# Attention and feed-forward block: values in runs of three units, other work paced by TensorE's columns and VectorE's reads

## The reference, cut to what matters

```python
xn = layernorm(x)
q, k, v = heads(xn @ Wq.T + bq), heads(xn @ Wk.T + bk), heads(xn @ Wv.T + bv)   # 16 heads of 16
q, k = rope(q), rope(k)
att = softmax(where(tril, q @ k.T / 4, -inf))
attn = merge(att @ v) @ Wo.T + bo
prob = softmax(xn @ router_w.T + router_b)        # 16 blocks of 64 hidden units
mask = the 4 best blocks of each token
h = relu(where(mask, xn @ w1.T + b1, 0))          # 1024 hidden units
out = x + attn + (h @ w2.T + b2)
```

## Time and profile before

| what | value |
|---|---|
| median of 3 runs | 927.0 us (926.43 to 928.52) |
| profiled execution | 931.0 us |
| its span, first to last instruction | 929.2 us |
| mean granted TensorE clock | 0.984 |
| TensorE, matmuls | 881.8 us busy |
| VectorE | 547.9 us busy |
| ScalarE | 458.3 us busy |
| GpSimd | 281.6 us busy |

### The profile page before, as it was taken

The page is one execution under the profiler, slowest core; times in us unless marked ns, Lnnn a source line. Parts: engine busy times, 40 slices in busy tenths (PEclk is TensorE's granted clock), DMA queues, the critical chain, the costliest instruction groups (busy, mean ns, idle before and its releaser), DMA issues.

```text
span 929.2 us, 15131 instructions
## 1 busy us (share of the span) xinstructions
PE 881.8 (95%) x5440; PEld 498.9 (54%) x5440; DVE 547.9 (59%) x1728; ACT 458.3 (49%) x1065; POOL 281.6 (30%) x298
## 2 busy tenths in 40 slices
PE   4879999999999999999999999999999999999996
PEld 2546544543555645555555655555555555565554
DVE  5936755667777565565666656555555765655301
ACT  2511355556555554445563554545454654645562
POOL 4356042916540029265041007627200002000000
PEclk9979999999999999999999999999999999999999
DMA  8570401423331144230230224122240205000001
GB/s 296 190 203 20 118 3 47 137 71 69 95 114 43 28 138 137 70 71 4 91 113 2 70 71 113 50 75 63 70 132 8 70 24 138 2 3 1 3 1 46
DMA packets 45626, 69.65 MB, mean 75 GB/s; under 512 B 5104, under 2 KB 20336, under 8 KB 45552
## 3 DMA queue, kind: packets, MB, share of 16 engines
q1 hardware_dynamic: 45552, 68.69, 25.4%
HBM read 38.93 MB, written 29.75 MB: 74 GB/s over the span
## 4 chain that ended last, share of the span: by engine, by line
PE 82%; DVE 7%; issue 5%; DMA 2%; ACT 2%; POOL 1%; SPq 1%; ACTq 0%; DVEq 0%; POOLq 0%
PE o_bank L887 14%; PE s_bank L871 14%; PE m_bank L821 13%; PE m_bank L810 12%; PE s_bank L797 11%; PE s_bank L771 5%; PE m_bank L858 3%; PE s_bank L874 3%; PE s_bank L780 2%; PE m_bank L836 1%; DVE m_bank L1101 1%; PE s_bank L801 1%; POOL x_sb L525 1%; DMA k_st<-term_scratch 1%; DMA term_scratch<-pieces 1%
## 5 line engine op out<-in xcount | busy, mean ns | idle before, releaser
L678 ACT ACTIVATE probs<-s_bank 128x512 f32<-128x512 f32 (+3 forms) x768 | 342.6, 492 | 250.1 <-PE s_bank L874 184.3
L821 PE MATMUL m_bank<-k_st,q_st 96*128 96x512 bf16 (+3 forms) x768 | 249.8, 330 | 13.9 <-DVE row_max L1101 5.7
L871 PE MATMUL s_bank<-q_st,k_st 99*128 99x512 bf16 (+3 forms) x768 | 250.0, 331 | 3.8 <-ACT rope_sb L640 2.2
L1098 DVE TENSOR_REDUCE part_max<-m_bank 128x1 f32<-128x512 f32 x256 | 167.5, 687 | 88.8 <-PE m_bank L821 87.6
L1101 DVE CUSTOM_DVE_ANT_0 m_bank<-m_bank,tri,part_max 128x512 f32<-128x512 f32 (+3 forms) x256 | 131.8, 556 | 68.9 <-PE m_bank L821 67.2
L887 PE MATMUL o_bank<-probs,v_sb 128*17 128x512 f32 (+3 forms) x1536 | 161.6, 494 | 0.0
L1101 DVE CUSTOM_DVE_ANT_0 m_bank<-m_bank,tri 128x512 f32<-128x512 f32 (+3 forms) x256 | 121.6, 512 | 54.3 <-PE m_bank L821 52.9
L871 PEld LDWEIGHTS s_bank<-q_st,k_st 99*128 99x128 bf16 x768 | 74.7, 97 | 142.5 <-ACT probs L678 70.2
L537 POOL TENSOR_SCALAR max_neg<-row_max 128x16 f32<-128x16 f32 x32 | 8.1, 254 | 470.1 <-DVE row_max L1101 470.1
L797 PE MATMUL s_bank<-xnT,w_sb 128*128 128x256 f32 x512 | 136.1, 389 | 0.2
L810 PE MATMUL m_bank<-w_sb,hT 128*128 128x256 f32 x512 | 123.4, 396 | 3.2 <-DVE row_max L1101 1.5
(11 more groups left out here) (81 smaller groups left out, 753.6 us busy)
## 6 DMA issues: line engine op xcount, KB each, us to landing
term_scratch<-pieces SPq DMA_DIRECT2D x96, 256.0 KB
q_st<-term_scratch SPq DMA_DIRECT2D x16, 768.0 KB, 5.7
k_st<-term_scratch SPq DMA_DIRECT2D x16, 768.0 KB, 8.5
acc<-in_x SPq DMA_DIRECT2D x8, 512.0 KB, 4.5
out<-acc SPq DMA_DIRECT2D x8, 512.0 KB, 2.9
x_sb<-in_x SPq DMA_DIRECT2D x3, 1024.0 KB, 6.6
x_sb<-in_x SPq DMA_DIRECT2D x2, 512.0 KB, 4.6
w_sb<-in_w1T SPq DMA_DIRECT2D x1, 1024.0 KB, 8.9
```

What stands on the lines that cost most here:

```text
L678: nc.scalar.activation(probs[:, u % P_SLOTS, h, 0:w], filled("score", n, k, h)[:, 0:w], ACT.Exp, scale=SCALE).then_inc(s_out, 1)
L821: nc.tensor.matmul(bank[:, 0:w], q_st[0:KROWS, at, h, i * P:(i + 1) * P], k_st[0:KROWS, at, h, c * HALF:c * HALF + w], start=True, stop=Tr ...
L871: last = nc.tensor.matmul(bank[:, 0:w], k_st[0:SROWS, at, h, j * P:(j + 1) * P], q_st[0:SROWS, at, h, q0:q0 + w], start=True, stop=not dia ...
L1098: ins = nc.vector.tensor_reduce(part_max[:, h, at:at + 1], bank[:, 0:w], AX.X, ALU.max)
```

## The change

Values are issued in runs: after the last head step of units 0, 3, 6 and 9 of a group, the three units before that one are issued one after the other (`pv_units`), instead of one unit, two behind, after each. `probs` has four slots instead of three. To make room, `yT` has no buffer of its own any more; it lies in the rope pair of even r, and ScalarE waits for GpSimd's last piece of r = 2 before it writes it.

`paced` counts, besides the pieces of work, what stands on TensorE anyway (`group_fixed`: scores, maxima, masks and runs of values), and it measures how far a group has got by what VectorE has to read, a unit's width plus 128, instead of by the width alone. So pieces of work move between units. The transposes of o and ScalarE's copies ahead of them move by one or two units: half 0 to (8, 1), half 1 to (2, 1) of the next group.

```diff
--- before.py
+++ after.py
@@ -49,8 +49,9 @@
         (7, 1, 512), (6, 1, 384), (5, 1, 256), (4, 1, 128)]
 HALF_OF = [i // 4 for i, c, w in MAXU]
 
-S_SLOTS, M_SLOTS, P_SLOTS, STACKS = 3, 3, 3, 3
-LAG = 2
+S_SLOTS, M_SLOTS, P_SLOTS, STACKS = 3, 3, 4, 3
+
+RUN = 3
 STACK_INC = 16 * 2
 PIECES_INC = 16 * 2 * NTERM
 
@@ -117,9 +118,9 @@
 
 def turns(n):
 
-    at = {(1, 1): [("maxT", n, 1)], (7, 0): [("oT", n, 0)]}
+    at = {(1, 1): [("maxT", n, 1)], (8, 1): [("oT", n, 0)]}
     if n:
-        at[3, 0] = [("oT", n - 1, 1)]
+        at[2, 1] = [("oT", n - 1, 1)]
     if n + 1 < GROUPS:
         at[8, 0] = [("maxT", n + 1, 0)]
     return at
@@ -173,25 +174,50 @@
     return w
 
 
-def paced(works, at, widths):
-
-    total, done, gone = sum(COST[what[0]] for _, what in works), 0, 0
+def width(k):
+
+    c, j = UNITS[k]
+    return (c + 1) * HALF - max(c * HALF, j * P)
+
+
+def pv_units(n, k):
+
+    u = n * NU + k
+    return range(u - RUN, u) if u and u % RUN == 0 else range(0)
+
+
+def paced(works, at, fixed):
+
+
+    read = [w + P for i, c, w in MAXU]
+    total = sum(COST[what[0]] for _, what in works) + sum(fixed)
+    done, gone = 0, 0
     for k in range(NU):
         for h in range(GH):
-            gone += widths[k]
+            gone += read[k]
+            done += fixed[k * GH + h]
             last = k == NU - 1 and h == GH - 1
             at.setdefault((k, h), [])
             while works and (last or works[0][0] <= k and done + COST[works[0][1][0]] / 2
-                             <= total * gone / (GH * sum(widths))):
+                             <= total * gone / (GH * sum(read))):
                 at[k, h].append(works[0][1])
                 done += COST[works.pop(0)[1][0]]
     return at
 
 
+def group_fixed(n):
+
+    columns = []
+    for k in range(NU):
+        for h in range(GH):
+            columns += [2 * width(k) + (P if diagonal(*UNITS[k]) else 0)]
+        columns[-1] += sum(4 * width(u % NU) for u in pv_units(n, k))
+    return columns
+
+
 FIRST_MAX = paced(after(0, ffn(0, 0, 1) + hid(0, 1, *range(FB)) + ffn(0, 2)),
-                  {(8, 0): [("maxT", 0, 0)]}, [w for i, c, w in MAXU])
-WORK = [paced(group_work(n // NG, n % NG), turns(n), [(c + 1) * HALF - max(c * HALF, j * P) for c, j in UNITS])
-        for n in range(GROUPS)]
+                  {(8, 0): [("maxT", 0, 0)]}, [w for i, c, w in MAXU for _ in range(GH)])
+WORK = [paced(group_work(n // NG, n % NG), turns(n), group_fixed(n)) for n in range(GROUPS)]
 
 NORMALISED = {0: 1, 3: 2, 7: 3}
 TURNED = {}
@@ -254,7 +280,6 @@
 
         x_sb = sb("x_sb", [P, NT, D])
         xnT = sb("xnT", [P, 2, KB, T])
-        yT = sb("yT", [P, KB, T])
         acc = sb("acc", [P, NT, D])
         wq_sb = sb("wq_sb", [P, KB, D])
         wk_sb = sb("wk_sb", [P, KB, D])
@@ -281,6 +306,7 @@
         probs = sb("probs", [P, P_SLOTS, GH, HALF])
         hT = sb("hT", [P, FB, QTR])
         rope_sb = sb("rope_sb", [P, 2, 2, T])
+        yT = rope_sb[:, 0]
         oT = sb("oT", [P, HALF])
         y_sb = sb("y_sb", [P, NT, D])
         b2_sb = y_sb[:, 0, :]
@@ -659,12 +685,14 @@
                 kb, h = u // 2, u % 2
                 if b and u == 0:
                     act.wait_ge(m_fill, M_COUNT["out", b - 1, 3])
+                if u == 0:
+                    act.wait_ge(low_done, chain(min(b + 1, B - 1), 2))
                 nc.scalar.activation(yT[:, kb, h * HALF:(h + 1) * HALF], filled("yT", b, u), ACT.Identity,
                                      bias=bv_sb[:, kb:kb + 1]).then_inc(s_out, 1)
 
             def take_o(n, c):
 
-                act.wait_ge(pv_done, n * NU + (4 if c == 0 else NU))
+                act.wait_ge(pv_done, n * NU + (2 * RUN if c == 0 else NU))
                 if n or c:
                     act.wait_ge(m_fill, M_COUNT[("oT", n, 0) if c else ("oT", n - 1, 1)])
                 nc.scalar.activation(oT[:], o_bank[:, c, :], ACT.Copy).then_inc(o_out, 1)
@@ -724,9 +752,9 @@
                         exp(n, k, h)
                         for what in WORK[n][k, h]:
                             take(what)
-                        if n and (k, h) == (2, 0):
+                        if n and (k, h) == (1, 0):
                             take_o(n - 1, 1)
-                        if (k, h) == (6, 0):
+                        if (k, h) == (7, 0):
                             take_o(n, 0)
             take_o(GROUPS - 1, 1)
             for what in LAST:
@@ -939,11 +967,12 @@
                         score(n, k, h)
                         if n + 1 < GROUPS:
                             max_unit(n + 1, k, h)
-                        if h == GH - 1 and n * NU + k >= LAG:
-                            pv(n * NU + k - LAG)
+                        if h == GH - 1:
+                            for u in pv_units(n, k):
+                                pv(u)
                         for what in WORK[n][k, h]:
                             work(what)
-            for u in range(GROUPS * NU - LAG, GROUPS * NU):
+            for u in pv_units(GROUPS, 0):
                 pv(u)
             for what in LAST:
                 work(what)
```

## The result

952.5 us, median of 4 runs (950.90 to 953.62), against 926.8 (926.43 to 928.52) for the kernel before: ratio 1.0273 [1.0254, 1.0291]. The forecast was 910, faster. The profiled execution took 951.7 us, span 949.9, against 931.0 and 929.2.

What follows compares the result with a forecast made beforehand. TensorE, busy 95%, was taken as the bound. 931.0 - 26.5 + 5.1 + 4.0 + 1.8 + 1.0 + 0.5 - 2.5 = 914.4 us profiled; the median lies 4.0 lower, so 910, range 899 to 920.

Steps and rivals of the forecast that it cites:

- (f): Pacing by VectorE's reads, whole kernel: takes away some of the present waits, -2.5 us, bounds 0 and 17.
- (a): Batch ends (groups 3, 7, 11): waits for VectorE's routing of 3.4 us, 1.7 more than before, 5.1 in all.
- (b): Units 1 to 3 of groups 1, 4, 8, 12: 3.2 us more waiting; groups 3, 7: some 0.4 each.
- (c): Six other group ends, units 10 and 11, without other work: waits of 0.5 instead of 0.2 us, 1.8 in all.
- (d): Group 15, with scores alone: runs of values bunch ScalarE's work; 1 us, bounds 0 and 3.
- (e): Group 0, the maxima's transpose: GpSimd's chain gets no shorter, so 0.5 us of the saving is waited there.
- main term: Entries into the values: 64 instead of 190, 126 x 0.21 = 26.5 us off TensorE's queue; joins cost nothing.
- Rival 4: At 128 joins between units, weight loads cannot run beside matmuls, about 0.10 us each: +12.8, 923 us; 3%.
- rival 3: TensorE's clock halves after the sparse stretches at batch ends, 5 to 10 us: 915 to 920 us; 18%.
- cost 0 as well: Moved o-transposes: issued five head steps behind their run, ScalarE's copy begun one step behind it, so 0 us.
- Rival 5: A run empties the buffers of maxima and scores, TensorE held to VectorE's pace: 952 us at 0.8 a run; 4%.
- Rival 2: New waits hardly come, three buffers and the pacing absorb them; only the routing's wait grows: about 901 us; 26%.

## Why the prediction was wrong

By its own steps; the measured column is the difference of gaps at the same units of the two traces, from starts, except for (f), which is the median with the new pacing alone less that of the kernel before.

| step | predicted | measured |
|---|---|---|
| 126 entries saved | -26.5 | -26.8 |
| (a) ends of batches, three | +5.1 | +5.4, and 6.2 of half clock behind them |
| (b) units 1 to 3 of groups 1, 4, 8, 12; of 3, 7 | +3.2; +0.8 | +2.9; +1.1 |
| (c) other group ends, units 10, 11 | +1.8 | +4.3 |
| (d) group 15 | +1.0 | +3.1 |
| (e) group 0, the maxima's transpose | +0.5 | +1.4 |
| (f) pacing by reads | -2.5 | -0.5, not told from 0 |
| units 8 and 9 of groups 0 to 14 | 0 | +10.6 |
| units 2 and 3 elsewhere | 0 | +4.9 |
| unit 1 of groups 2, 6, 10 | 0 | +3.9 |
| unit 0 of groups 5, 6, 9, 10 | 0 | +2.7 |

All other units together come to about -0.4, so that the gaps sum to +39.9.

- **The main term was right to 0.3 us**: entries and exits, and the joins, which cost 2 to 3 ns each. Rival 4 is refuted.
- **The wait at the batch ends was right, its clock was not in the sum.** 3.4 us were forecast for each and 3.9 measured. I had the clock as rival 3, 5 to 10 us for the three, and it was 6.2 there; but I held it against the wait as an alternative, where it follows from it. 5.1 us more of half clock stand behind waits in groups 0, 6 and 10, where I had put no clock at all.
- **The step that failed is the list of waits (a) to (f), and the cost of 0 for everywhere else.** I looked for units where work was missing and the present trace already waited, found (a) to (c), and put everywhere else at zero. The last four lines of the table are 22.1 us at units that I had put at nothing. (c), (d) and (e) were seen but taken too small: 8.8 us for a forecast of 3.3. Of the four lines, units 8 and 9 (most of it) and units 2 and 3 grow with the old pacing too; unit 1 and unit 0 grow only with the new pacing on top of the runs. The list also started from a miscount: runs stand behind four of the twelve units, so at two of three units nothing is left between the maxima, where the prediction says three of four.

  Units 8 and 9 are the largest. The transpose of o's first half now stands at (8,1), one head step behind the maxima's transpose, whose copy VectorE makes only after the maxima ahead of it. Where no work lies between the two transposes, the second waits for a buffer. I had called the o-transposes "cost 0 as well" by looking at whether their input was ready, not at who holds their buffer:

```profile
440.42 0.24 PE L856 MATMUL m_bank<-identb,max_pc 128*48 128x128 bf16 x1
...
441.60 0.63 PE L864 MATMUL m_bank<-ident,oT 128*128 128x128 f32 x4 [0.35 <-DVE max_pcT L1139]
442.06 3.62 PE L838 MATMUL m_bank<-w_sb,hT 128*128 128x256 f32 x16
```

  Behind the feed-forward tile of 442.06 TensorE gets through a head step of 384 columns in 0.40 us and VectorE in 0.54; without values between them the third and the next tile wait, 0.7 us in all. At unit 1 of groups 2, 6 and 10 a stream shuffle of 1.4 us on VectorE holds up the next maximum and the small copy behind it:

```profile
406.03 1.38 DVE L1066 STREAM_SHUFFLE rope_sb<-rope_sb 128x1024 f32<-128x1024 f32 x1
407.28 0.59 DVE L1130 CUSTOM_DVE_ANT_0 m_bank<-m_bank,tri 128x384 f32<-128x384 f32 x1
```

and on TensorE, at the same time:

```profile
406.22 0.34 PE L849 MATMUL m_bank<-k_st,q_st 96*128 96x384 bf16 x1
407.98 4.33 PE L838 MATMUL m_bank<-w_sb,hT 128*128 128x256 f32 x11 [1.42 <-DVE max_pcT L1139]
```

  At unit 0 of groups 5, 6, 9 and 10 a projection now stands directly ahead of short head steps, and the score waits for ScalarE's copy out of the buffer:

```profile
399.73 0.38 PE L899 MATMUL s_bank<-q_st,k_st 99*128 99x512 bf16 x1 [0.52 <-ACT rope_sb L666]
```

- **Rival 5 was the right one, at 4%.** It named the run that empties three buffers, with the price of 0.8 us a run at 952. Measured: 39.9 + 7.3 = 47.2 us over 64 runs in the two traces, 0.74 us a run, and 52.5 us or 0.82 by the medians, against the 0.41 from which it decides. The 0.8 was an example and not worked out, so that its 952 meets 952.5 is luck. Its mechanism needs two corrections. It names both rings, and the traces show both (31.0 us in front of VectorE's, 10.4 in front of ScalarE's), but its pace is VectorE's alone. TensorE is not held to VectorE's average pace for a whole group; it is held up at single places, by narrow units and by pieces of fixed length, several times a group. My argument against it was the feed-forward tile of 3.6 us, behind which TensorE hardly waits. That was true of the tile but not of a run: behind the tile in the kernel before came head steps with values between them. As I read it, a long block is harmless where slack is spread behind it; the runs took away that slack at two of three units and made it into long blocks.
- **Rival 2** (the buffers absorb it, since VectorE is busy 59% only) was wrong for the same reason: a share of 59% says nothing of whether 0.5 us is there each time it is needed.
- **The pacing** was not the helper I took it for. Alone it gives nothing; with runs it costs 9.4 us. It counts a run as work done, so that work moves ahead of the run or further behind it, though VectorE has just idled under the run (2.01 us in the row at 283.74).

What stays open: how much of the 9.4 us each placement of the new pacing makes (the profiles show +7.0 us of gaps, 6.5 of them at the two places named above, and no run moved them one by one); what in ScalarE's order makes the 10 us in front of the scores' ring; what the fourth slot of `probs` and yT's new buffer cost, which every run with values in runs has; and whether a fourth buffer of maxima would take up the runs, which was not tried. The tables of places are one choice each; what a better one for each run length would give is not known, so the 7.2 us between runs of three and single units holds for these tables alone.

## What to carry to other kernels

Before gathering small pieces of work into a block, ask what they cover where they stand. Here the saving on the bound engine's queue was lost where a place without its filler had too little work to outlast the next engine's longest fixed piece, with a ring of three buffers between them. Look at every ring that the block empties, not only at that of the busier engine. Cost each such place from both engines' starts, all of them and not only those that wait today, and add the clock to each wait instead of treating it as another case. Where the bound engine waits for short, frequent service, placing the filler well can be worth more (30 to 39 us here) than the entries saved (27).

## What the runs showed of the hardware

- Going into values that use four column strips of 32 costs 97 ns and coming out 117 ns, at every undisturbed place of both traces; a join between two units in the strips costs 2 to 3 ns. By the Trainium skill ("TensorEngine Tiling (Array Packing)", Key Properties) a change of tiling mode drains TensorE, with no price given; these two numbers are what the change in and out costs in this kernel.
- At a batch end after, two waits of 1.1 and 1.6 us, with TensorE busy for 3.85 of 6.60 us, were followed by 3.4 us at half clock; before, TensorE was busy for 4.66 of 5.50 us there and the granted clock stayed at 1.00. So the waits at a batch end, 3.9 us measured, cost 5.5 with the clock (extra 1.6 us), and 7.0 in the third, where the half clock lasted 6.8 us.
- Not every wait meets the clock: in the profiled execution with the routing moved, 101.5 us of gaps in groups left one half-clock stretch behind 142 us; with the o-transposes moved as well, 95.8 us left none. Nor does it meet the same waits each time: executions of one kernel (the one with the routing moved) had mean granted clocks of 0.987 and 0.991.
